# A decoder layer on one core: the triangular inverse laid out along its summed index, moved within the step, with five moves beside it

## What is computed

```python
x = layernorm(x + attn(x))          # gated delta rule, 32 value heads on 16 key heads of 128
x = layernorm(x + xattn(x, ctx))    # 32 query heads of 8 channels on a short context
x = layernorm(x + moe(x))           # 7 routed experts, top 2, and one shared
```

```python
Sm = Sm * exp(g);  delta = (v - k @ Sm) * beta
Sm = Sm + outer(k, delta);  o = q @ Sm
```

## Time and profile before

| | |
|---|---|
| median of 3 runs | 2256.93 us (2249.43 to 2257.33) |
| the profiled execution, its time | 2255.11 us |
| its span in the profile | 2253.2 us |
| PE busy | 2091.6 us (93%) |
| DVE busy | 1711.3 us (76%) |
| ACT busy | 1512.7 us (67%) |
| POOL busy | 904.1 us (40%) |
| granted clock of PE, mean | 0.970 |

### The profile page before, as it was taken

One profiled execution on the slowest core, in us unless ns is written; L12 is line 12 of the kernel. 1 busy time (PEld: TensorE's weight loads), 2 busy tenths in 40 slices (PEclk: granted clock), 3 DMA queues, 4 the chain that ended last, 5 costly groups with the idle time before them and its releaser, 6 DMA issues.

```text
span 2253.2 us, 49295 instructions
## 1 busy us (share of the span) xinstructions
PE 2091.6 (93%) x18636; PEld 1716.1 (76%) x18636; DVE 1711.3 (76%) x2944; ACT 1512.7 (67%) x3585; POOL 904.1 (40%) x714
## 2 busy tenths in 40 slices
PE   4659999999999999999999999999988899999998
PEld 4448888888888888888888888887776476666776
DVE  6789797887879788787977978787325777767665
ACT  4547777777777777777777677775767666565632
POOL 1534454444445445445535534532333123213232
PEclk8779999999999999999999999998999999999999
DMA  3432322322232332233233222212243012322232
GB/s 77 94 73 48 89 44 72 63 64 67 55 85 46 72 75 49 68 60 80 52 70 72 48 70 56 75 34 56 58 137 133 1 66 76 104 94 73 91 136 85
DMA packets 274633, 161.56 MB, mean 72 GB/s; under 512 B 209352, under 2 KB 246752, under 8 KB 269280
## 3 DMA queue, kind: packets, MB, share of 16 engines
q1 hardware_dynamic: 274400, 158.41, 27.6%
HBM read 122.43 MB, written 35.91 MB: 70 GB/s over the span
## 4 chain that ended last, share of the span: by engine, by line
issue 36%; POOL 26%; PE 23%; DVE 8%; ACT 4%; DMA 2%; SPq 2%; POOLq 0%; DVEq 0%; ACTq 0%
POOL SM L577 5%; POOL EB L493 5%; POOL Q L555 5%; PE ps L1739 4%; POOL SZ L579 3%; PE ps L1347 3%; POOL EB L497 3%; PE ps L1349 3%; PE ps L1348 3%; POOL WL L471 2%; POOL SM L585 2%; PE ps L1660 1%; ACT SC L856 1%; PE ps L1651 1%; PE ps L1480 1%
## 5 line engine op out<-in xcount | busy, mean ns | idle before, releaser
L909 DVE SCALAR_TENSOR_TENSOR A<-ps,CW,A 128x508 f32<-128x508 f32 (+2 forms) x768 | 515.9, 734 | 55.3 <-ACT A L671 50.1
L572 POOL TENSOR_SCALAR SM<-SM 128x8 f32<-128x8 f32 x64 | 12.6, 196 | 813.8 <-ACT DL L690 813.8
L1480 PE MATMUL ps<-WO,DL 128*128 128x256 f32 x1008 | 244.5, 394 | 39.5 <-POOL WO L484 24.5
L1480 PEld LDWEIGHTS ps<-WO,DL 128*128 128x128 f32 x1008 | 189.7, 194 | 74.5 <-POOL WO L484 26.4
L1347 PE MATMUL ps<-XH,WH 128*128 128x512 f32 x512 | 221.5, 433 | 26.7 <-DVE A L909 25.8
L1127 DVE TENSOR_TENSOR SZ<-SZ,ps 128x512 f32<-128x512 f32 x128 | 87.7, 687 | 201.5 <-PE ps L1514 201.4
L1349 PE MATMUL ps<-XH,WL 128*128 128x512 f32 x512 | 206.4, 403 | 0.0
L1348 PE MATMUL ps<-XL,WH 128*128 128x512 f32 x512 | 205.2, 401 | 0.0
L690 ACT ACTIVATE DL<-SZ 128x128 f32<-128x128 f32 x512 | 152.4, 298 | 38.5 <-PE ps L1514 28.8
L856 ACT ACTIVATE SC<-ps,A 128x128 f32<-128x128 f32 x512 | 141.7, 386 | 51.5 <-DVE A L1252 50.7
L1112 DVE TENSOR_TENSOR BP<-ps,EB 128x512 f32<-128x512 f32 x256 | 158.3, 681 | 3.3 <-ACT EB L665 3.3
(11 more groups left out here) (225 smaller groups left out, 5556.1 us busy)
## 6 DMA issues: line engine op xcount, KB each, us to landing
EB<-decay_rows SPq DMA_DIRECT2D x128, 256.0 KB, 4.7
WE<-expert_halves SPq DMA_DIRECT2D x32, 1024.0 KB, 5.1
x_blocks<-BP SPq DMA_DIRECT2D x256, 32.0 KB, 1.7
X<-x_blocks SPq DMA_DIRECT2D x16, 512.0 KB, 6.5
tt_blocks<-TI SPq DMA_DIRECT2D x16, 512.0 KB, 2.6
tn_blocks<-TM SPq DMA_DIRECT2D x16, 512.0 KB, 2.6
TTF<-tt_blocks SPq DMA_DIRECT2D x256, 32.0 KB, 1.9
expert_halves<-BP SPq DMA_DIRECT2D x8, 1024.0 KB, 5.8
```

The source lines that it names most:

```text
L909: dve.scalar_tensor_tensor(acc, ps(i, 0, [[128, 4], [1, 128 - s]]), at(CW, tile * 4 + 3 - s, [[1, 1]]), acc, ALU.mult, ALU.add).then_inc(s ...
L1480: t = pe.matmul(ps(7 - i, b * 256, [[1, 256]]), at(on_buf(k), (4 * i + 2 * b + v) * 128, [[1, 128]]), at(WO, v * 256, [[1, 256]]), start=( ...
```

## The change

1. **Layout.** Sizes 8 and 16 of the last two products are computed with the summed index innermost in TM, so that each reduce reads consecutive words. For this one operand of each product has to lie transposed. ACT makes transposed copies of two parts of X once per inverse (`mirror`, two activations, which wait for X to have landed), at n%4 == 0 between z_silu and the first v_tap3. DVE makes two small transposed copies of TI. The inverse has 43 instructions where it had 41.
2. **Place.** In steps with s3 and s1 (n = 8 to 63) the room in front of the v_taps falls from 2500 + 1560 to 2000, and the room in front of the gate rises from 2000 to 4200.
3. **The copy of TI for TA** moves from ACT to POOL, behind decay and ahead of the chain L572.
4. **scale_wo** moves to the end of the step before (k%4 == 3, n%4 == 0), ahead of the chain L572; load_wo moves to the end of SP's list of that step. The pow for the keys (L585) moves from behind that chain to ahead of it.
5. **The first eight steps.** kq_proj of odd groups uses banks 4 and 5, so it no longer waits for the taps of the group before; ACT makes kq_tap3(n+1) ahead of the silu of group n.

```diff
-INV_OPS = 41
+INV_OPS = 43
...
+        def kq_bank(n):
+            return 4 if n < 8 and n % 2 else 0
...
@@ SP, loop over n
-                    if 0 < k < NSTEP and k % 4 == 0:
-                        load_wo(k // 4)
                     if n % 4 == 0 and 4 <= n <= NSTEP:
                         load_x(n // 4 - 1)
...
                     if n + 3 < NSTEP:
                         load_rows(n + 3)
+                    if 0 <= k and k % 4 == 3 and k + 1 < NSTEP:
+                        load_wo(k // 4 + 1)
                     if n == NSTEP + 1:
...
@@ POOL, loop over n
-                    if 0 < k < NSTEP and k % 4 == 0:
-                        scale_wo(k // 4)
                     if EARLY - 1 <= n and n + 2 < NSTEP:
                         decay(n + 2)
...
+                    if n % 4 == 0 and 4 <= n <= NSTEP:
+                        ...
+                        pool.tensor_tensor(at(SM, C_SK + (j % 2) * 16, [[4, 4], [1, 4]]), at(SM, C_NK, [[4, 4], [1, 4]]),
+                                           at(SM, C_PH, [[0, 4], [1, 4]]), ALU.pow).then_inc(sem["sk"], 1)
+                    if 0 <= k and k % 4 == 3 and k + 1 < NSTEP:
+                        scale_wo(k // 4 + 1)
+                    if sv and vn % 4 == 0:
+                        pool.wait_ge(sem["inv"], INV_OPS * (vn // 4 + 1))
+                        pool.tensor_copy(at(TM, 0, [[1, 32], [32, 32]]), at(TI, 0, [[32, 32], [1, 32]])).then_inc(sem["tn"], 1)
...
@@ ACT
-                    back = n - 2 if n < 6 else n - 1
+                    back = n - 2 if n <= 6 else n - 1
...
+                def mirror(j):
+                    act.wait_ge(sem["ld_xb"], 16 * (j + 1))
+                    act.activation(at(X, 8 * 32, [[528, 2], [32, 8], [1, 8]]), at(X, 8, [[528, 2], [1, 8], [32, 8]]),
+                                   ACT.Copy).then_inc(sem["x_mir"], 1)
+                    act.activation(at(X, 16 * 32, [[32, 16], [1, 16]]), at(X, 16, [[1, 16], [32, 16]]),
+                                   ACT.Copy).then_inc(sem["x_mir"], 1)
...
+                    if n < 6:
+                        kq_tap3(n + 1)
                     if s1:
                         act.wait_ge(sem["kq_conv"], 6 * n + 6)
...
+                    if n % 4 == 0 and 4 <= n <= NSTEP:
+                        mirror(n // 4 - 1)
                     if sv:
                         v_tap3(vn, 0)
...
-                    if sv and vn % 4 == 0:
-                        act.wait_ge(sem["inv"], INV_OPS * (vn // 4 + 1))
-                        act.activation(at(TM, 0, [[1, 32], [32, 32]]), at(TI, 0, [[32, 32], [1, 32]]), ACT.Copy).then_inc(sem["tn"], 1)
...
@@ DVE, inverse(j)
-                    for s in (2, 4, 8):
+                    for s in (2, 4):
...
+                    dve.wait_ge(sem["x_mir"], 2 * j + 1)
+                    for it in range(2):
+                        dve.wait_ge(inv, done)
+                        dve.tensor_tensor(at(TM, it * 512, [[64, 8], [8, 8], [1, 8]]), at(TI, it * 528, [[32, 8], [0, 8], [1, 8]]),
+                                          at(X, it * 528 + 256, [[0, 8], [32, 8], [1, 8]]), ALU.mult).then_inc(inv, 1)
+                        ...
+                        yield 612
+                    dve.tensor_reduce(at(UT, 0, [[1, 128]]), at(TM, 0, [[8, 128], [1, 8]]), AX.X, ALU.add).then_inc(inv, 1)
+                    yield 1124
+                    dve.tensor_copy(at(X, 0, [[528, 2], [32, 8], [1, 8]]),
+                                    at(TI, 8 * 33, [[528, 2], [1, 8], [32, 8]])).then_inc(inv, 1)
+                    yield 228
+                    ...
+                    dve.wait_ge(sem["x_mir"], 2 * j + 2)
                     for q4 in range(4):
...
-                        dve.tensor_reduce(at(UT, k0, [[1, 4], [16, 16]]), at(TM, 0, [[16 * kn, 4], [1, 16], [16, kn]]), AX.X,
-                                          ALU.add).then_inc(inv, 1)
+                        dve.tensor_reduce(at(UT, k0 * 16, [[1, 64]]), at(TM, 0, [[kn, 64], [1, kn]]), AX.X, ALU.add).then_inc(inv, 1)
...
+                    dve.tensor_copy(at(X, 0, [[32, 16], [1, 16]]), at(TI, 16 * 33, [[1, 16], [32, 16]])).then_inc(inv, 1)
+                    yield 356
...
@@ DVE, loop over n
-                    pump(2500)
-                    pump(1560)
+                    pump(2000 if s3 and s1 else 4060)
...
-                    pump(2000)
+                    pump(4200 if s3 and s1 else 2000)
                     if s3:
                         gate(m, 0)
...
@@ PE, kq_proj(n)
+                        elif n >= 2:
+                            pe.wait_ge(sem["kq_conv"], 6 * (n - 2) + 5 + i)
                         elif n:
-                            pe.wait_ge(sem["kq_conv"], 6 * (n - 1) + 5 + i)
+                            pe.wait_ge(sem["ab"], 4)
...
-                        proj(i, W_KQ + 128 * i, n % 4).then_inc(sem["kq_proj"], 1)
+                        proj(kq_bank(n) + i, W_KQ + 128 * i, n % 4).then_inc(sem["kq_proj"], 1)
```

More of the change, by code:

```diff
@@ L659, in kq_tap3 @@
                         act.wait_ge(sem["kq_proj"], 2 * n + 1 + i)
-                        act.activation(at(kq_buf(n), i * 512, [[1, 512]]), ps(i), ACT.Copy,
+                        act.activation(at(kq_buf(n), i * 512, [[1, 512]]), ps(kq_bank(n) + i), ACT.Copy,
                                        scale=at(CW, tile * 4 + 3, [[1, 1]])).then_inc(sem["kq_tap3"], 1)
@@ L901, in _, with tap @@
             def _(dve):
-                def tap(name, n, buf, tiles, s):
+                def tap(name, n, buf, tiles, s, bank=0):
                     for i, tile in enumerate(tiles):
@@ L935, in inverse @@
                         dve.wait_ge(sem["st_tn"], 16 * j)
-                    for s in (2, 4, 8):
+                    for s in (2, 4):
                         nb, blk = 16 // s, 66 * s
                         mid = ([s * s, nb * s], [1, s], [s, s])
-                        for it in range(min(nb, s)):
-                            if nb <= s:
+                        for it in range(s):
+                            if nb == s:
                                 o, xo, to = it * s ** 3, it * blk + s, it * blk
@@ L970, in inverse @@
                         yield 100 + nb * s * s * s
+                    dve.wait_ge(sem["x_mir"], 2 * j + 1)
[3 more added lines that the diff above has]
+                                          at(X, it * 528 + 256, [[0, 8], [32, 8], [1, 8]]), ALU.mult).then_inc(inv, 1)
+                        done += 1
+                        yield 612
+                    dve.wait_ge(inv, done)
+                    dve.tensor_reduce(at(UT, 0, [[1, 128]]), at(TM, 0, [[8, 128], [1, 8]]), AX.X, ALU.add).then_inc(inv, 1)
+                    done += 1
+                    yield 1124
+                    dve.tensor_copy(at(X, 0, [[528, 2], [32, 8], [1, 8]]),
+                                    at(TI, 8 * 33, [[528, 2], [1, 8], [32, 8]])).then_inc(inv, 1)
+                    done += 1
+                    yield 228
+                    for it in range(2):
+                        dve.wait_ge(inv, done)
+                        dve.tensor_tensor(at(TM, it * 512, [[64, 8], [8, 8], [1, 8]]), at(UT, it * 64, [[8, 8], [0, 8], [1, 8]]),
+                                          at(X, it * 528, [[0, 8], [32, 8], [1, 8]]), ALU.mult).then_inc(inv, 1)
+                        done += 1
+                        yield 612
+                    dve.wait_ge(inv, done)
+                    dve.tensor_reduce(at(TI, 8, [[528, 2], [32, 8], [1, 8]]), at(TM, 0, [[8, 128], [1, 8]]), AX.X, ALU.add,
+                                      negate=True).then_inc(inv, 1)
+                    done += 1
+                    yield 1124
+                    dve.wait_ge(sem["x_mir"], 2 * j + 2)
                     for q4 in range(4):
@@ L1618, in _ @@
                                 pe.wait_ge(sem["delta"], 2 * m + 1 + b // 2)
+                            elif b == 0:
+                                pe.wait_ge(sem["kq_conv"], 6 * 8)
                             for v in range(2):
```

39 lines of the change are left out of this document (18 added, 21 removed).

## The result

The changed kernel takes 2275.86 us (median of six runs, 2260.76 to 2280.72) against 2257.13 before: ratio 1.0074, 95% interval 1.0055 to 1.0093. The medians differ by 18.7 us. The profiled execution has a span of 2277.3 us, 24.1 more than that of the kernel before; the times of the changed kernel go with the granted clock (mean 0.964 to 0.972), which turns out to be part of the story.

A forecast was written before the change was run, and what follows sets the result against it. PE was taken to bound the steady steps, DVE the first inverse. +0.4 us per four steps times 14 = +6, and -14 elsewhere, made -8 against 2255.1: 2247, so a median of 2249 us, range 2222 to 2270.

The forecast's parts named there:

- The mirror: Steps with n%4 == 0: ACT waits 1.6 us for X, so PE waits 1.5 us; bounds 0 and 2.5.
- the gains of 2.3: Per four steady steps: 0.9 us from taking the transposed copy off ACT, 1.4 from moving scale_wo.
- the copy for TA on POOL: Behind decay on POOL: costs 2.0 us (bounds 1.04 and 3.0); X lands at 1043.6 instead of 1041.3.
- rival (a): POOL's copy cheap (1.04 us; first rule: only wide-step reads are dear) or X in time: median 2231, chance 0.34.
- Room in front of the gate: Steps with n%4 == 0: DVE's longer list delays the gate, PE waits 1.2 us; bounds 0.4 and 2.1.
- scale_wo earlier: PE's wait for scaled w_out goes: -1.4 us per four steps, and 7.4 us near the end.
- Layout: DVE's reduces: 1.2 us for 1024 terms, not 2.1; 3.2 per last set, not 5.1; 4.5 saved per inverse.
- the first eight steps: Projection no longer waits for taps, but ACT's silu waits behind kq_tap3: 0, bounds -3 and +3 us.
- The end: Last inverse (n = 64, 65) -2.5 us, and PE's 7.4 us wait for the scaled w_out gone.
- The sum: Whole kernel: +0.4 us per four steps, times 14 = +6; outside -14; together -8.
- first inverse: 96 to 152 us, where DVE is the bound: the shorter reduces give -4 us.
- Rival (b): DVE becomes the bound at n%4 == 0, gate late or POOL's copy dear: 2271 (2282 with both), chance 0.14.

The follow-up runs named there:

- e1_tn_act: The changed kernel with the transposed copy of TI for TA moved back from POOL to ACT: 2240.62 us, ratio 0.9939 to the kernel before.
- e1_wo_only: The kernel before with only load_wo and scale_wo moved one step earlier: 2274.54 us, ratio 1.0083.
- e2_wo_sk: The kernel before with load_wo and scale_wo one step earlier and POOL's power for sk put in front of scale_wo: 2263.26 us, ratio 1.0040.
- e4_best2: The changed kernel with mirror behind u2_copy, rooms and first eight steps as in the kernel before, TA copy ending DVE's inverse: 2226.11 us, ratio 0.9864.
- e2_idle6: The kernel before with six repeated ACT copies ahead of the first u2_copy in steps with n%4 == 0, so PE idles: 2275.45 us, ratio 1.0087.
- e3_idle12: The kernel before with twelve repeated ACT copies ahead of the first u2_copy in steps with n%4 == 0: 2362.84 us, ratio 1.0482.
- e4_best3: As e4_best2, but with the mirror in front of v_tap3, where the change has it: 2268.88 us, ratio 1.0064.
- e2_tn_dve: The changed kernel with the transposed copy of TI as the last operation of DVE's inverse instead of on POOL: 2270.32 us, ratio 1.0058.

## Why the prediction was wrong

Two steps of the working failed. The mirror's wait was sized at 1.5 us and was 2.3. And every wait of PE was priced at its own length, with nothing for the clock behind it, which cost as much as 22 us. Term by term, per four steps: the gains of 2.3 came, the mirror costs 2.3, the gate 0.8, the clock at most 1.7, together 2.5 where 0.4 was forecast and 2.7 was measured (100.3 less 97.7).

- **The direction of the copy for TA on POOL** was right: 2.00 us as forecast, not L566's 1.04, so for this write the first rule of rival (a), by which only reads are dear, is no guide. The second, a penalty for whoever crosses lines, fits POOL and ACT (2.03), but DVE makes the same copy in 1.12 us. load_x goes out 2.5 us later in the median step (2.9 in step 43) against 2.3 forecast, 9.8 after the TN store against 10.2 less 1.1.
- **The mirror** is the first term that failed, in size: 2.3 us a step (30.3 in 13), not 1.5, inside its bounds. Its own two copies took 1.05 us as forecast (1.0); X's landing took 7.1 us in the median, and 8.5 in step 44, not 6.5. The 0.6 of the landing and the 0.2 of load_x make up the 0.8. Why it lands more slowly wasn't tried; e1_tn_act has 6.3.
- **What a wait of PE costs** is the step that was missing. I priced a wait at its own length. Behind 7 of the 13 waits for u2_copy (1.8 to 4.0 us long) PE ran at granted clock 0.5, 1.2 GHz: at most 22 us over the kernel, 1.7 per four steps.
- **Room in front of the gate**: 10.2 us in the 13 steps up to 1500 us, 0.8 a step against 1.2.
- **scale_wo earlier**: the 1.4 us per four and the 7.4 at the end came, but by luck. I followed the late chain to on_tr and not to what stands behind it on POOL, the power for sk, squares and decay. The move alone costs 19 us (e1_wo_only), with the power in front of it 6 (e2_wo_sk); in the changed kernel that power and, by what the runs allow, the shorter list of DVE pay for it. That DVE and POOL slow each other I had used for POOL alone.
- **Layout**: reduces of 1024 took 1.22 us (forecast 1.2) and those of the last size 410 to 420, 686, 953 and 1220 ns, 3.3 us for a set (forecast 3.2). DVE is busy 78 us less. Up to step 8 the kernel without the new order of the first eight steps gains 6.4 us (5.5 in e4_best2; forecast 4), which **the first eight steps** take back: I put them at 0, bounds -3 and +3, and they cost 5 to 6 there; step 5 starts 7.5 us later, and the net at step 8 is -0.4.
- **The end**: from step 63 on the changed kernel regains 11.8 us (forecast 9.9).
- **The sum**: steady 36 us over steps 8 to 63 instead of 6, and first inverse -0.4 instead of -4. With the end that is the 32 us between -8 and +24, the latter by the profiled executions; by the medians it is +19, or 27 us over the forecast. Rival (b) had the right step and a near result (2271, its sum 2282), but another mechanism: it put the loss at the gate, for which PE waited less than even the forecast had it, and in the price of the copy, which was 2.0. I gave all of the slower side 0.17, since I had priced each new wait within a narrow band and none of them could multiply.

The version to keep is the changed kernel with the mirror behind u2_copy and the rooms of the kernel before (e2_mir_rooms): 0.9864, 1.4% under it.

## What to carry to other kernels

An instruction put in front of others in an engine's list brings its wait along, as the mirror did here: ask when its operand lands as well as what it costs, and place it where everything behind it can wait. A wait of the engine that sets the pace is not priced at its length once its clock falls behind it: here 14 waits of 1.3 us cost 18 us and 14 of 3.7 us cost 108, so (an estimate from these two) three short waits are cheaper than one of their sum. And when one of several moves looks like a gain by itself, ask which of the others makes it one: moving scale_wo alone loses 19 us, with the power for sk 6, and none of the three kernels with the old layout came out ahead, while with the new one eight kernels did, once no wait for X stood in front of u2_copy or X was in time.

## What was unexpected of the hardware

Of 26 idle times of PE of 1.3 us (e2_idle6, 200 to 1500 us) one was followed by 3.4 us at granted clock 0.5, and 25 left it at 1.0. Those of 3.7 us came each time with a stretch at 0.5, mostly of 10.2 us (e3_idle12), and those of 2.3 us on average with 3.4 or 6.8 us in about every second step (the changed kernel). The time of one and the same kernel goes with the clock: 12 executions of e4_best3 took 2253.85 (mean clock 0.970) to 2281.51 us (0.964). A DVE product of two SBUF tensors took 1943 ns instead of 692 beside POOL's chain, a reduce 2052 instead of the 2.11 us of the earlier trace rows. And the transposed copy of 1024 words costs 2.00 us on POOL, 2.03 on ACT, and 1.08 (e4_best3) to 1.12 on DVE, 1.38 in e2_tn_dve.
